# Six local-attention layers on one core: a new order of each engine's work, probabilities turned in place, keys with a copied prefix, and inner features padded to a full chunk

## The reference, cut to what matters

```python
def attn_layer(x, Wqkv, qs, ksc, Wo):
    q, k, v = split into 16 heads of 64
    q = l2norm(q) * qs;  k = l2norm(k) * ksc          # then rotary tables
    out = local_attention(q, k, v)                    # window 64, looks one window back
    return out @ Wo
def ffn_layer(x, g, bln, W1, b1, W2, b2):             # layer norm, then
    a, gate = split(xn @ W1 + b1)                     # 682 inner features each
    return a * gelu(gate) @ W2 + b2
for i in range(6):
    x = attn_layer(shift_tokens(x), ...) + x
    x = ffn_layer(shift_tokens(x), ...) + x
```

## Time and profile before

| | us |
|---|---|
| median of 3 runs | 4176.97 (4171.86 to 4179.23) |
| the profiled execution | 4173.6, its span 4171.8 |
| PE busy | 3999.7 (96%) |
| DVE, ACT, POOL busy | 2980.7, 2635.9, 2069.8 |
| the six local layers | from about 1257 to the end |

### The profile page before, as it was taken

One profiled execution on the slowest core, in us unless ns is written; L12 is line 12 of the kernel. 1 busy time (PEld: TensorE's weight loads), 2 busy tenths in 40 slices (PEclk: granted clock), 3 DMA queues, 4 the chain that ended last, 5 costly groups with the idle time before them and its releaser, 6 DMA issues.

```text
span 4171.8 us, 97939 instructions
## 1 busy us (share of the span) xinstructions
PE 3999.7 (96%) x33244; PEld 2841.6 (68%) x33244; DVE 2980.7 (71%) x5352; ACT 2635.9 (63%) x7072; POOL 2069.8 (50%) x1371
## 2 busy tenths in 40 slices
PE   6999988999678999999999999999999999999998
PEld 3666545665355777777777777777777777777777
DVE  4888547887787777777767776677767777777775
ACT  3677534777535676767666666767666666666665
POOL 1000001000137666666666666666666666666774
PEclk8999998999779999999999999999999999999999
DMA  6111132221103000110011100120011100111110
GB/s 161 37 44 42 25 113 68 55 53 32 61 19 116 21 19 21 59 45 19 21 41 44 38 19 22 51 53 22 19 30 51 42 19 21 53 50 23 23 26 24
DMA packets 103536, 177.53 MB, mean 43 GB/s; under 512 B 27541, under 2 KB 62129, under 8 KB 102961
## 3 DMA queue, kind: packets, MB, share of 16 engines
q1 hardware_dynamic: 102320, 169.70, 15.3%
q0 software_dynamic: 768, 2.10, 0.4%
HBM read 94.93 MB, written 23.07 MB: 28 GB/s over the span
## 4 chain that ended last, share of the span: by engine, by line
PE 68%; issue 1%; POOL 0%; DMA 0%; DVE 0%; ACT 0%; POOLq 0%; DVEq 0%; ACTq 0%; SPq 0%
PE PS L2281 23%; PE PS L2389 10%; PE PS L2367 8%; PE PS L2405 7%; PE PS L2356 5%; PE PS L2328 4%; PE PS L2337 4%; PE PS L2291 2%; PE PS L2301 2%; PE PS L2393 1%; PE PS L2376 1%; PE PS L2267 1%; PE PS L2323 0%; POOL rinv L2200 0%; POOL swp L2190 0%
## 5 line engine op out<-in xcount | busy, mean ns | idle before, releaser
L938 DVE TENSOR_REDUCE maxima<-PS 128x1 f32<-128x512 f32 x1024 | 632.4, 681 | 123.1 <-PE PS L772 122.7
L2226 POOL TENSOR_TENSOR probs<-probs,prob_recip 128x512 f32<-128x512 f32 x384 | 486.7, 1286 | 467.0 <-DVE prob_recip L2668 466.5
L2281 PE MATMUL PS<-wqk,xT 128*128 128x512 f32 x1536 | 711.0, 596 | 3.8 <-DMA wqk<-in_L_ffn_Wqkv 2.6
L2190 POOL TENSOR_TENSOR swp<-raw,table 128x512 f32<-128x512 f32 x384 | 651.7, 1708 | 0.7 <-DVE ss L2610 0.6
L902 ACT ACTIVATE probs<-PS 128x512 f32<-128x512 f32 x1024 | 520.0, 603 | 154.9 <-PE PS L786 154.2
L2539 ACT ACTIVATE probs<-probs,neg 128x128 f32<-128x128 f32 x1536 | 596.3, 402 | 1.3 <-DVE neg L2662 0.2
L2200 POOL TENSOR_TENSOR rinv<-ssm,power 128x32 f32<-128x32 f32 x96 | 531.4, 5535 | 66.9 <-DVE ssm L2617 66.7
L2281 PEld LDWEIGHTS PS<-wqk,xT 128*128 128x128 f32 x1536 | 286.3, 191 | 329.4 <-issue 324.4
L2389 PEld LDWEIGHTS PS<-xnT,w 128*128 128x128 f32 x3840 | 458.7, 192 | 45.7 <-issue 45.6
L2389 PE MATMUL PS<-xnT,w 128*128 128x128 f32 x3840 | 475.3, 275 | 0.9 <-issue 0.9
L772 PE MATMUL PS<-k_stack,q_stack 112*128 112x512 f32 (+1 forms) x1024 | 430.5, 442 | 35.6 <-PEq L640 18.9
(11 more groups left out here) (282 smaller groups left out, 7872.1 us busy)
## 6 DMA issues: line engine op xcount, KB each, us to landing
V_window<-V SPq DMA_DIRECT2D x180, 256.0 KB, 3.6
wqk<-in_L_ffn_Wqkv SPq DMA_DIRECT2D x12, 1024.0 KB, 5.2
w<-in_L_ffn_W SPq DMA_DIRECT2D x18, 640.0 KB
q_stack<-spin_qk SPq DMA_DIRECT2D x128, 80.0 KB
k_stack<-spin_qk SPq DMA_DIRECT2D x128, 80.0 KB
q_stack<-tok_qk SPq DMA_DIRECT2D x128, 64.0 KB, 2.7
k_stack<-tok_qk SPq DMA_DIRECT2D x128, 64.0 KB, 2.8
spin_qk<-shared SPq DMA_DIRECT2D x32, 256.0 KB
```

Of the source, the lines that this page charges most:

```text
L938: dve.tensor_reduce(maxima[:, k // 2, k % 2:k % 2 + 1], SM(r, k), AX.X, ALU.max).then_inc(sm_maxed, 1)
L2190: pool.tensor_tensor(swp[:, w, :, a:a + LD // 2], raw[:, w, :, b:b + LD // 2], table[:, j % 2, 2 + w, a:a + LD // 2].rearrange("p (o d) -> ...
L2226: pool.tensor_tensor(view, view, psr[:, 4 * q:4 * q + 4].rearrange("p (h o) -> p h o", o=1) .to_broadcast([P, 4, P]), ALU.mult).then_inc(p ...
L2281: mm = pe.matmul(wide(kind, half, j), xT[:, k, at:at + P], rhs, start=(k == 0), stop=(k == DC - 1))
```

## The change: what it does

- Every engine's `step` list gets a new order and new lags, the deepest lag goes from 7 to 6, and the PSUM job lists are written to match. On PE, `scores(0)`, `scores(1)`, `weigh(0)`, `weigh(1)` now stand in a row; before, the two scores stood between the two weighings. SP's list, which loads weights and shifts rows, is reordered too.
- `pT` is gone. `take_p` writes a turned quarter back over the quarter of `probs` that it came from, and `weigh` reads it there. `mask_scores` of the next tile therefore waits for `pv_done` (the weighing) and no longer for `p_done` (the transpose).
- `kT` gets 64 more columns in front. When the last tile of the ring is taken, ACT copies its last 64 keys there too, and `scores` has one form for all tiles.
- The last chunk of `ffn_out` multiplies all 128 rows. Rows 42 to 127 of `hidden` and of `w2` are set to zero once at the start, by two more memsets on POOL.

```diff
-        kT = c.sb(ctx, "kT", [P, PAIRS, 4 * P])
+        kT = c.sb(ctx, "kT", [P, PAIRS, WINDOW + 4 * P])
-        pT = c.sb(ctx, "pT", [P, 2, 4 * P])
...
-        T_JOBS = [("xn", 0, 6), ("x", 0, 1), ("kt", 0, 3), ("p", 0, 4), ("kt", 1, 3), ("p", 1, 4), ("qt", 1, 3), ("qt", 0, 3), ("p", 2, 4), ("p", 3, 4), ("o", 0, 4), ("o", 1, 4)]
+        T_JOBS = [("x", 0, 0), ("qt", 0, 2), ("p", 0, 3), ("qt", 1, 2), ("kt", 1, 2), ("kt", 0, 2), ("p", 3, 3), ("p", 1, 3), ("p", 2, 3), ("o", 0, 3), ("o", 1, 3), ("xn", 0, 4)]
...
-                                lo = at + (v - 1) * WINDOW
-                                if v == 0 and j % 4 == 0:
-                                    pe.matmul(out[:, 0:WINDOW], lhsT, kT[rows, s, 4 * P - WINDOW:4 * P],
-                                              start=True, stop=True, skip_group_check=True)
-                                    mm = pe.matmul(out[:, WINDOW:P], lhsT, kT[rows, s, 0:WINDOW],
-                                                   start=True, stop=True, skip_group_check=True)
-                                else:
-                                    mm = pe.matmul(out, lhsT, kT[rows, s, lo:lo + P], start=True, stop=True, skip_group_check=True)
+                                lo = at + v * WINDOW
+                                mm = pe.matmul(out, lhsT, kT[rows, s, lo:lo + P], start=True, stop=True, skip_group_check=True)
...
-                                mm = pe.matmul(bank[w * LD:(w + 1) * LD, at:at + WINDOW], vals, pT[:, w, at:at + WINDOW],
+                                mm = pe.matmul(bank[w * LD:(w + 1) * LD, at:at + WINDOW], vals, probs[:, 4 * (2 * u + w) + i, v * WINDOW:(v + 1) * WINDOW],
...
-                        rows = P if f < W2C - 1 else TAIL1
-                        mm = pe.matmul(FFN, hidden[0:rows, j % 2, f, :], w2[0:rows, f, :], start=(f == 0), stop=(f == W2C - 1),
+                        mm = pe.matmul(FFN, hidden[:, j % 2, f, :], w2[:, f, :], start=(f == 0), stop=(f == W2C - 1),
...
-                    act.activation(kT[:, 4 * half:4 * half + 4, (j % 4) * P:(j % 4 + 1) * P], turned("kt", half, j).rearrange("p (i t) -> p i t", i=4),
-                                   ACT.Copy).then_inc(kt_taken[half], 1)
+                    ins_ = act.activation(kT[:, 4 * half:4 * half + 4, at:at + P], src, ACT.Copy)
+                    if j % 4 == 3:
+                        ins_ = act.activation(kT[:, 4 * half:4 * half + 4, 0:WINDOW], src[:, :, P - WINDOW:P], ACT.Copy)
+                    ins_.then_inc(kt_taken[half], 1)
...
-                    wait(dve, p_done[q], n)
+                    wait(dve, pv_done[q // 2], n)
...
-                    wait(dve, pv_done[1 - q // 2], n + q // 2)
-                    dve.tensor_copy(pT[:, 0, :], turned("p", q, j)).then_inc(p_taken[q], 1)
+                    dve.tensor_copy(probs[:, 4 * q:4 * q + 4, :], turned("p", q, j).rearrange("p (i k) -> p i k", i=4)).then_inc(p_taken[q], 1)
```

More of the change, by code:

```diff
@@ L2421, in step @@
+                    if t2:
+                        transpose_k(t2, 0)
                     if t5:
-                        project_out(t5)
+                        ffn_in(t5, 1)
                     if t3:
-                        project(t3, "v", 1)
+                        transpose_p(t3, 3)
+                    if t3:
+                        transpose_p(t3, 1)
+                    if t3:
+                        transpose_p(t3, 2)
                     if t2:
-                        project(t2, "q", 1)
@@ L2427, in step @@
-                    if t6:
-                        ffn_in(t6, 2)
+                        scores(t2, 0)
+                    if t2:
+                        scores(t2, 1)
                     if t3:
-                        transpose_k(t3, 0)
+                        weigh(t3, 0)
+                    if t3:
+                        weigh(t3, 1)
+                    if t5:
+                        ffn_out(t5)
+                    if t1:
+                        project(t1, "v", 1)
+                    if t0:
+                        project(t0, "q", 0)
@@ L2459, in step @@
-                    if t6:
-                        ffn_out(t6)
+                        project_out(t3)
+                    if t1:
+                        project(t1, "v", 0)
                 steps(pe, step)
@@ L2557, in step @@
                 def step(t, i, l):
-                    t1, t2, t3, t4, t5, t6 = (stage(t, i, l, lag) for lag in (1, 2, 3, 4, 5, 6))
+                    t0, t1, t2, t3, t4, t5 = (stage(t, i, l, lag) for lag in (0, 1, 2, 3, 4, 5))
+                    if t4:
+                        take_o(t4, 0)
+                    if t4:
+                        take_o(t4, 1)
+                    if t3:
+                        exponentials(t3, 0)
+                    if t2:
+                        take_v(t2, 1)
@@ L2585, in step @@
-                    if t6:
-                        gelu(t6, 1)
-                    if t3:
-                        take_k(t3, 0)
-                    if t3:
-                        take_k(t3, 1)
-                    if t6:
-                        gelu(t6, 0)
-                    if t4:
-                        take_p(t4, 1)
-                    if t2:
-                        take_qk(t2, 0, 0)
-                    if t4:
-                        take_p(t4, 3)
+                        take_qk(t1, 0, 1)
@@ new lines, in step @@
+                    if t3:
+                        exponentials(t3, 1)
+                    if t0:
+                        take_x(t0)
+                    if t2:
+                        take_v(t2, 0)
+                    if t3:
+                        exponentials(t3, 2)
+                    if t5:
+                        gelu(t5, 1)
+                    if t1:
+                        take_qk(t1, 1, 0)
+                    if t1:
+                        take_qk(t1, 1, 1)
+                    if t2:
+                        take_k(t2, 1)
@@ L2599, in _ @@
+                    if t5:
+                        gelu(t5, 0)
+                    if t2:
+                        take_k(t2, 0)
+                    if t3:
+                        take_p(t3, 3)
+                    if t3:
+                        take_p(t3, 1)
                 steps(act, step)
@@ L2809, in step @@
                         moments(t4, 1)
+                    if t2:
+                        take_q(t2, 1)
+                    if t1:
+                        sum_squares(t1, 1)
+                    if t4:
+                        moments_ready(t4)
+                    if t5:
+                        gate(t5, 0)
+                    if t4:
+                        aggregate(t4)
+                    if t1:
+                        floor_squares(t1)
+                    if t3:
+                        take_p(t3, 2)
+                    if t4:
+                        variance(t4)
+                    if t1:
+                        cosines(t1, 0)
+                    if t2:
+                        mask_scores(t2, 0)
+                    if t4:
+                        standardise(t4)
+                    if t2:
+                        mask_scores(t2, 2)
+                    if t2:
+                        maxima(t2, 0)
+                    if t2:
+                        mask_scores(t2, 3)
+                    if t5:
+                        finish(t5)
+                    if t2:
+                        mask_scores(t2, 1)
+                    if t2:
+                        maxima(t2, 3)
+                    if t1:
+                        add_sines(t1, 0)
+                    if t2:
+                        invert_sums(t2, 0)
+                    if t2:
+                        maxima(t2, 1)
+                    if t1:
+                        cosines(t1, 1)
+                    if t1:
+                        normalise(t1, 0)
+                    if t2:
+                        maxima(t2, 2)
                 steps(dve, step)
```

234 lines of the change are left out of this document (81 added, 153 removed).

## The result

The changed kernel takes 4115.05 us (median of 4 runs, 4111.19 to 4120.08), the kernel before, measured beside it, 4175.77 (4171.86 to 4179.23). The ratio is 0.9856, with a 95% interval from 0.9842 to 0.9871: 60.7 us faster.

The account below looks back on a forecast made before the run. PE was taken as the bound, busy in all of each 29.79 us step. Terms 32.9 + 14.4 + 4.8 = 52.1, less 2.5 and 2, gave about 47 us: 4177 - 47 = 4130, range 4117 to 4152.

Parts of the forecast that it names:

- The jumps back: PE's idle 16.6 us from first to last ffn_out, read as the hardware loop's three jumps; no gain forecast.
- cheaper jumps: Part of the low end of the forecast's own range, 4118, together with term 2 at 0.20.
- The fill: Start of the local layers: one step shorter in count but not work, 0; first loads reordered, within 2 us either way.
- Term 1: Last chunk of ffn_out padded from 42 to 128 rows: 0.34 us a step gone, 32.9 us in all.
- The rival: Against term 1: the 42 rows cost nothing of themselves, term 1 is 0, time 4163; chance 0.05.
- Term 2: Both scores ahead of both weighings on PE: one change of shape fewer, 0.15 us a tile, 14.4 us.
- Term 3: Copied key prefix in kT, scores no longer split: 0.20 us on 24 of 96 tiles, 4.8 us.
- ACT's loop: PE to ACT to PE, before probability quarter 2's transposes: about 0.7 us left, nothing at prefix steps; charged 2 us.
- the first rival: ACT late in every step, not only prefix steps: a 0.25 us stall a tile costs 24 us, 4154; chance 0.10.
- The drain: Last five tiles wait on other engines, so half a microsecond less PE work each shows only in part: 2.5 us.
- The added wait of the masks: mask_scores on DVE waits for the weighing; costed at nothing, covered by ffn_out (2.6 us).
- the slower rival: Single probs buffer becomes the bound: PE stalls once its chain is 3.4 us longer; at 4.4, time 4226; chance 0.05.

Follow-up runs that it names:

- the kernel with the three parts: Kernel before with the jump back moved behind project_out, the padded last chunk of ffn_out and the copied key prefix: 4117.08 us, ratio 0.9855.

## Why the prediction missed, point by point

- **The jumps back: the step that failed.** The prediction read "of which PE is idle 16.6: that is the three jumps back of the hardware loop", and then took every term from the steps between them. Even the reading was right by chance alone: 10.2 us of the idle time are at the jumps, 6.4 in the drain, and the jumps cost 6.4 us more in which PE is busy, mostly at the lower clock. The jumps were carried over into the forecast unchanged; only the range's low end had "cheaper jumps". The new list ends behind `project_out` and v, with 4.6 us of queued records against a jump of about 4, and all 16.6 us are gone. The move of the cut alone is worth 18 us in the kernel before by its medians, 16.6 by its steps, 12.3 by its local stretch with fill and drain. The information was there: the change in PE's list showed which pieces stand last, and the wait rows at the jump showed what they must cover.
- **The fill.** "Within 2 us either way" was mis-sized: loading k third costs one wait of 3.36 and a slower start, 4.8 us net in the fill, 6.8 against q, k, v. It took back not quite a third of what the jumps gave. "One step shorter in count but not in work" named no wait, and PE's wait for `wqk` is the one that mattered.
- **Term 1**, 32.9: measured 31.7 alone, 0.34 a step as read. The rival rested on the Trainium skill, page TensorE: Matmul & The Clock Gate, section LDWEIGHTS: a weight load takes the same time for 32 rows as for 128. For the load itself the trace agrees (42-row and 128-row loads of `ffn_out` both last 0.18 to 0.19 us); the time is lost in the gaps around it, which that sentence leaves out.
  The Trainium skill, page TensorEngine Tiling (Array Packing), section Key Properties, has the rule on the other side: changing the tiling mode drains the engine. Free 106 rows and dear 64 and 42 agree with it; no row shows a drain as such.
- **Term 2**, 14.4: 0.155 a change where it was put back, and 0.14 to 0.15 a step between the kernel with the three parts and the kernel after. One change isn't like the other: by starts, the one out of the scores costs 0.16, the others 0.09 to 0.10, each before what its own first group adds.
- **Term 3**, 4.8: measured 4.3 alone by medians, the steps of 29.99 are gone.
- **ACT's loop**: 0.7 of room predicted, 0.53 measured by filling it, nothing left at the prefix steps as predicted; charged at 2 us, it costs 0.01 to 0.04 on the steps concerned, well under 1 us in all. A first stall was half a microsecond away in each ordinary step, and the first rival's 0.25 some 0.8.
- **The drain**: charged at 2.5 us; the five draining steps gained 0.7 where five of 0.54 would be 2.7, so 2.0.
- **The added wait of the masks, and the single buffer of probabilities** cost nothing: PE has no wait between 1400 and 4000 us. The loop that was to decide the slower rival never showed, and what is left of its 3.4 us of room wasn't tried.

## What to carry to other kernels

When a change rewrites the list of a hardware loop, look at which instructions stand last before the jump: on the engine that bounds the kernel, a taken jump wanted some 4 us of queued work ahead of it here, and rotating the list adds no work (though a few us came back in fill and drain). An engine's idle time behind its own jump costs nothing while it doesn't bound. Count the changes of TensorE's shape in a step, some 0.15 us each at float32 here, and pad a tail of zeros to the full array: at 64 rows the tail still cost 0.39 us. Price an uncovered jump with a spread: in the old order it cost 4.9 to 6.7 us, more where the clock stayed low for longer. Where a change is bundled, price the fill as its own term, from the waits of the first pieces, and not as a remainder.

## What the runs showed of the hardware

- A taken jump back held PE's queue for 3.3 to 4.3 us in every kernel, one not taken 76 ns. On ACT, DVE, POOL and SP the same records last 40 to 74 ns, but on ACT, POOL and DVE the next record of the queue comes 2.4 to 3.1 us after a taken jump (0.1 after the one not taken). The length of the record is not the price.
- In the old order PE's queue paused again behind the first or second record after the jump, for 2.3 to 2.9 us, with no semaphore to wait for.
- After about 4 us in which PE was almost idle, its granted clock was 0.50 (1.2 GHz) for 3.4 or 6.8 us and then 1.00 again, so a jump that isn't covered costs more than its gap: 5.5 us a jump, of which the waits are 3.4. Behind gaps of 0.7 to 0.9 us it stayed at 1.00.
- One pair of 64-row records among 128-row ones cost 0.39 us a step, one of 42 rows 0.34, and one of 106 nothing.
- Steps with 3, 4 and 5 changes between 128x128, 64x64 and 128x64 shapes take 29.30, 29.45 and 29.61 us.
